# A two-layer transformer block on one core: the windowed attention's VectorE work in operations of 1024 columns, and new orders of the steps

## The reference, cut to what matters

```python
Kw = Kp[:, :, idx]                       # idx: position l sees l-3 .. l+3 (zeros beyond the ends)
scores = jnp.einsum('bhld,bhlwd->bhlw', Q, Kw) / np.float32(np.sqrt(DH))
attn = jax.nn.softmax(scores, axis=-1)
fw = attn * conn                         # conn: one weight for each head and shift, from a small network
fw = fw / (fw.sum(axis=-1, keepdims=True) + 1e-09)
out = jnp.einsum('bhlw,bhlwd->bhld', fw, Vw)
```

## Time and profile before

| | |
|---|---|
| median of 3 runs | 1133.05 us (1133.0 to 1134.91) |
| profiled execution | 1138.12 us, span 1136.3 us |
| granted TensorE clock, mean | 0.954 |
| PE busy | 1003.8 us (88%) |
| DVE busy | 943.6 us (83%), 2536 instructions |
| ACT busy | 752.2 us (66%) |

### The profile page before, as it was taken

How to read it: one execution, slowest core, us unless ns; L and a number is a source line. 1 busy time by engine, 2 the same in 40 slices (tenths; PEclk the granted TensorE clock), 3 DMA queues, 4 the chain that set the end, 5 groups by cost and what they waited for, 6 DMA issues and landing times.

```text
span 1136.3 us, 20042 instructions
## 1 busy us (share of the span) xinstructions
PE 1003.8 (88%) x7166; PEld 713.5 (63%) x7166; DVE 943.6 (83%) x2536; ACT 752.2 (66%) x1854; POOL 145.5 (13%) x400
## 2 busy tenths in 40 slices
PE   4877789999999999999999999999999898888652
PEld 2655557676867676767777676857676666565321
DVE  3877676689898989898998989998999896868854
ACT  2233554758686877768686778686877778577653
POOL 2001100101102020202011111102020202010000
PEclk8778999999999999999999999999999999999875
DMA  7821123011111202030303021120202000000000
GB/s 210 328 83 53 31 74 93 1 49 36 47 56 30 73 24 79 10 93 10 93 3 91 11 63 40 38 65 29 75 19 75 10 11 19 2 20 1 10 10 10
DMA packets 36627, 58.91 MB, mean 52 GB/s; under 512 B 6784, under 2 KB 15872, under 8 KB 36016
## 3 DMA queue, kind: packets, MB, share of 16 engines
q1 hardware_dynamic: 36528, 57.64, 16.4%
HBM read 28.65 MB, written 4.19 MB: 29 GB/s over the span
## 4 chain that ended last, share of the span: by engine, by line
PE 40%; DVE 39%; ACT 15%; issue 4%; POOL 2%; DMA 0%; SPq 0%; ACTq 0%; DVEq 0%; POOLq 0%
PE bank_c L447 15%; PE bank_e L447 6%; PE bank_a L447 5%; DVE area_f L1240 5%; DVE area_a L980 5%; DVE neg_top L1173 4%; DVE area_a L1024 3%; ACT squares_out L1314 3%; PE bank_f L447 3%; PE bank_x L447 3%; DVE x L878 2%; ACT area_e L1509 2%; DVE area_f L1231 2%; ACT area_f L1538 2%; DVE area_a L1028 2%
## 5 line engine op out<-in xcount | busy, mean ns | idle before, releaser
L1240 DVE SCALAR_TENSOR_TENSOR area_f<-area_f,w_convw 128x254 f32<-128x254 f32 x256 | 111.9, 478 | 9.3 <-ACT area_f L1538 7.0
L1302 ACT ACTIVATE area_bx<-bank_x 128x512 f32<-128x512 f32 (+1 forms) x144 | 69.9, 497 | 47.4 <-PE bank_x L641 22.0
L1173 DVE TENSOR_REDUCE neg_top<-bank_e 128x4 f32<-128x512 f32 x128 | 80.5, 681 | 10.1 <-PE bank_e L447 9.7
L1538 ACT ACTIVATE area_f<-area_f,w_convb,w_convw 128x256 f32<-128x256 f32 x128 | 69.9, 595 | 27.8 <-DVE area_f L1231 27.7
L980 DVE TENSOR_TENSOR area_a<-area_a 128x512 f32<-128x512 f32 x112 | 73.0, 682 | 14.0 <-ACT area_a L1302 13.1
L1024 DVE TENSOR_TENSOR area_a<-area_a 128x512 f32<-128x512 f32 x112 | 74.5, 684 | 0.9 <-DMA area_a<-area_a 0.7
L1302 ACT ACTIVATE area_a<-bank_a 128x512 f32<-128x512 f32 (+1 forms) x80 | 44.0, 550 | 41.2 <-PE bank_a L447 29.9
L1509 ACT ACTIVATE area_e<-bank_e 128x512 f32<-128x512 f32 x128 | 68.7, 594 | 1.4 <-PE bank_e L800 1.4
L1302 ACT ACTIVATE area_bx<-bank_c 128x512 f32<-128x512 f32 x64 | 34.5, 538 | 50.1 <-PE bank_c L447 47.6
L1028 DVE TENSOR_TENSOR area_a<-area_a 128x512 f32<-128x512 f32 x96 | 65.7, 684 | 0.2
L447 PE MATMUL bank_e<-area_e,chosen_v 128*32 128x512 f32 x256 | 57.2, 618 | 3.6 <-ACT area_e L1509 2.9
(11 more groups left out here) (307 smaller groups left out, 2716.6 us busy)
## 6 DMA issues: line engine op xcount, KB each, us to landing
area_a<-area_a SPq DMA_DIRECT2D x96, 224.0 KB
area_a<-in_xT SPq DMA_DIRECT2D x16, 256.0 KB, 2.9
x<-in_x SPq DMA_DIRECT2D x16, 256.0 KB, 2.8
area_bx<-in_ctxT SPq DMA_DIRECT2D x16, 256.0 KB, 2.7
area_d<-in_ctxT SPq DMA_DIRECT2D x16, 256.0 KB, 2.7
y<-x SPq DMA_DIRECT2D x16, 256.0 KB, 2.2
w_wqkv_e<-in_wqkv_e SPq DMA_DIRECT2D x1, 3072.0 KB, 11.0
area_f<-in_raw SPq DMA_DIRECT2D x2, 1024.0 KB, 9.9
```

The lines of the kernel that those rows point to most:

```text
L1173: dve.tensor_reduce(top[:, b, :, r, 0].rearrange("p (par c) -> p c par", c=DC), bank_e[r][:, :].rearrange("p (c par k) -> p c par k", c=DC ...
L1240: last = dve.scalar_tensor_tensor(c4[:, i, :, dst], h4[:, i, :, src], cwt3[:, 2 * jj + i, k:k + 1], c4[:, i, :, dst], ALU.mult, ALU.add)
L1302: return act.activation(dst, src, ACT.Copy)
L1538: last = act.activation(c4[:, i], h4[:, i], ACT.Identity, bias=w["convb"][:, j:j + 1], scale=cwt3[:, j, 1:2])
```

## The change

1. The five product buffers become one tile, and VectorE's products are made in four operations: shifts 0 and 2 at once, 4 and 6 at once, 1 alone, 3 and 5 at once. An operation for two shifts has 1024 columns: the queries are read twice, the keys by a pattern that begins again two positions on. PE waits for the second and the fourth of them.
2. The weighing is done in four operations (shifts 0 and 1, 2 and 3, 4 and 5, then 6), and the additions in four: a "first" of 1024 columns that adds shifts 0, 1 to 2, 3 into `prods`, one of 1024 columns for 4 and 5, one of 512 for 6, and a last that adds the two halves of 512. Each addition waits for the operation just issued ahead of it on behalf of the station.
3. `e0` is laid out by shift, sequence and head. So the sums over shifts (L1002, L1007) read with a step of 32 numbers instead of 16.
4. The order strings of all engines but POOL (where one letter pair moves) are new.

```diff
-WINDOWS = (0, 2, 4, 6, 1, 3, 5)
-SUM_STEPS = ((3,), (0,), (2,), (3, 0), (4,), (3, 2), (6,), (3, 4), (1,), (3, 6), (5,), (3, 1), (3, 5))
+PRODUCT_STEPS = ((0, 2), (4, 6), (1,), (3, 5))
+VALUE_STEPS = (("weigh", 0, 2), ("weigh", 2, 4), ("first", 0, 2), ("weigh", 4, 6), ("add", 4, 2), ("weigh", 6, 7), ("add", 6, 1),
+               ("last",))
...
-                for windows, made in ((WINDOWS[:4], 4), (WINDOWS[4:], 7)):
-                    pe.wait_ge(a_prod, WIN * g + made)
+                for windows, made in ((WINDOWS[:4], 2), (WINDOWS[4:], 4)):
+                    pe.wait_ge(a_prod, 4 * g + made)
...
+                    dve.tensor_tensor(prods[:, place:place + n, :].rearrange("p w (n t) -> p w n t", t=P),
+                                      bc(qT0.rearrange("p c (b t) -> p (c b) t", t=P), 1, n), shifted, ALU.mult).then_inc(a_prod, 1)
...
+                for step in VALUE_STEPS:
+                    if step[0] == "weigh":
+                        lo, hi = step[1:]
+                        v4 = vw[:, lo:hi, :].rearrange("p w (n d) -> p w n d", d=DH)
+                        weights = e0.rearrange("p (w n) -> p w n", w=WIN)[:, lo:hi, :]
+                        m = own.mark(dve.tensor_tensor(v4, v4, bc(weights, 3, DH), ALU.mult))
+                    elif step[0] == "first":
+                        dve.wait_ge(own.sem, m)
+                        m = own.mark(dve.tensor_tensor(prods[:, 0:2, :], vw[:, 0:2, :], vw[:, 2:4, :], ALU.add))
+                    elif step[0] == "add":
+                        lo, n = step[1:]
+                        dve.wait_ge(own.sem, m)
+                        m = own.mark(dve.tensor_tensor(prods[:, 0:n, :], prods[:, 0:n, :], vw[:, lo:lo + n, :], ALU.add))
```

More of the change, by code:

```diff
@@ L1 @@
+import itertools
 from contextlib import ExitStack
@@ L87 @@
[L87 to L91, removed]
@@ L211, in build @@
         kT0 = carve(DC * GB * LP).rearrange("p (c b t) -> p c b t", c=DC, b=GB)
-        prods = [carve(W2) for _ in range(5)]
+        prods = carve(5 * W2).rearrange("p (w n) -> p w n", n=W2)
         vw = carve(WIN * W2).rearrange("p (w n) -> p w n", w=WIN)
@@ L352, in product_of @@
         def product_of(wi):
-            return prods[WINDOWS.index(wi) % len(prods)]
+            return prods[:, WINDOWS.index(wi) % 5, :]
         block = ctx.enter_context(nc.Block())
@@ L991, in windowed @@
                 scores = bank_a[:, 0:GB * WH].rearrange("p (b w h) -> p b w h", b=GB, w=WIN)
-                e4 = e0.rearrange("p (b w h) -> p b w h", b=GB, w=WIN)
-                e_head = e4.rearrange("p b w h -> p b h w")
-                mx, den1, den2 = (den0[:, i, :].rearrange("p (b h) -> p b h", b=GB) for i in range(3))
+                e4 = e0.rearrange("p (w b h) -> p w b h", b=GB, w=WIN)
+                e_head = e0.rearrange("p (w n) -> p n w", w=WIN)
+                mx = den0[:, 0, :].rearrange("p (b h) -> p b h", b=GB)
                 m = own.mark(dve.tensor_reduce(mx, scores.rearrange("p b w h -> p b h w"), X, ALU.max))
                 dve.wait_ge(own.sem, m)
-                dve.tensor_tensor(e4, scores, bc(mx, 2, WIN), ALU.subtract).then_inc(a_shifted, 1)
+                dve.tensor_tensor(e4, scores.rearrange("p b w h -> p w b h"), bc(mx, 1, WIN), ALU.subtract).then_inc(a_shifted, 1)
                 yield
@@ L1001, in windowed @@
                 dve.wait_ge(a_exp, g + 1)
-                m = own.mark(dve.tensor_reduce(den1, e_head, X, ALU.add))
+                m = own.mark(dve.tensor_reduce(den0[:, 1, :], e_head, X, ALU.add))
                 dve.wait_ge(own.sem, m)
-                m = own.mark(dve.tensor_tensor(e0.rearrange("p (b n) -> p b n", b=GB), e0.rearrange("p (b n) -> p b n", b=GB),
-                                               bc(conn[:, :], 1, GB), ALU.mult))
+                m = own.mark(dve.tensor_tensor(e4, e4, bc(conn[:, :].rearrange("p (w h) -> p w h", w=WIN), 2, GB), ALU.mult))
                 dve.wait_ge(own.sem, m)
-                m = own.mark(dve.tensor_reduce(den2, e_head, X, ALU.add))
+                m = own.mark(dve.tensor_reduce(den0[:, 2, :], e_head, X, ALU.add))
                 dve.wait_ge(own.sem, m)
@@ L1012, in windowed @@
                 dve.wait_ge(own.sem, m)
-                dve.tensor_tensor(e4, e4, bc(mx, 2, WIN), ALU.mult).then_inc(a_fw, 1)
+                dve.tensor_tensor(e4, e4, bc(mx, 1, WIN), ALU.mult).then_inc(a_fw, 1)
                 yield
@@ L1016, in windowed @@
                 dve.wait_ge(a_fw, g + 1)
-                made = {}
-                for step in SUM_STEPS:
-                    if len(step) == 1:
-                        (wi,) = step
-                        v4 = vw[:, wi, :].rearrange("p (b h d) -> p b h d", b=GB, h=H)
-                        made[wi] = own.mark(dve.tensor_tensor(v4, v4, bc(e4[:, :, wi, :], 3, DH), ALU.mult))
-                    else:
-                        to, wi = step
-                        dve.wait_ge(own.sem, max(made[to], made[wi]))
-                        added = dve.tensor_tensor(vw[:, to, :], vw[:, to, :], vw[:, wi, :], ALU.add)
-                        if step == SUM_STEPS[-1]:
-                            added.then_inc(a_summed, 1)
-                        else:
-                            made[to] = own.mark(added)
+                for step in VALUE_STEPS:
[11 more added lines that the diff above has]
+                        m = own.mark(dve.tensor_tensor(prods[:, 0:n, :], prods[:, 0:n, :], vw[:, lo:lo + n, :], ALU.add))
+                    else:
+                        dve.wait_ge(own.sem, m)
+                        dve.tensor_tensor(prods[:, 0, :], prods[:, 0, :], prods[:, 1, :], ALU.add).then_inc(a_summed, 1)
                     yield
```

81 lines of the change are left out of this document (43 added, 38 removed).

## The result

The changed kernel took 1140.59 us (median of 7 runs, 1136.63 to 1141.18); the kernel before, beside it, 1134.43 us (1132.54 to 1136.75). The ratio is 1.0044, 95% interval 1.0030 to 1.0058: **slower by 0.44%**, 5.0 us (3.4 to 6.6), where 1130 was forecast. The medians themselves stand 6.2 us apart.

A forecast was written before the change was run, and what follows sets the result against it. PE (96% busy) and DVE (92%) were taken to bound each middle period in alternating halves. Terms -3, +1, +1, -2 gave -3 us: 1135.1 against the profiled 1138.12, so a 1130 us median; range 1124 to 1138.

The forecast's parts named there:

- hole on PE: PE ahead of C.dq, with E.aT moved behind it: up to 0.45 us open a period, at most +3.6, taken as +1.
- DVE's share: DVE over the whole run: 5.9 us less work, about half of it counting, -2 to -3.5 us, taken as -3.
- new waits on a predecessor: DVE's additions right behind what they need: 0.11 us a group, +1.8, and +1.3 us in groups 0 to 3.
- Fixed cost of an operation: DVE's column-independent cost, 0.07 us, saved when two operations become one: 0.56 us a group, 9.0 us in all.
- rival 4: DVE's merged pairs each save 0.138 us, 17.7 us in all, half on the path: 1124 us; chance 0.04.
- The new orders: Engines' step orders: win back part of PE's 27 us of idle time over 11 periods, counted as -2 us.
- a head that moves by more than 3 us: Stretch ahead of 240 us: nothing counted there, so a larger move would make the prediction wrong altogether.
- Coarser steps: Steps behind double operations on DVE: C.norm 0.26 us later, +1 over the run; E.att1 0.4 to 1.0 later, covered.
- Rival 2: PE's path: late C.norm and the open 0.45 us ahead of C.dq make it slower, 1137 up to 1141; chance 0.22.
- The period: Middle, between two F norms: 61.59 us read; 61.3 to 61.6 expected, above 61.9 would decide for slower.
- The layout of e0: DVE's sums over shifts, read with a step of 32 instead of 16: no change taken from 540 ns.

The follow-up runs named there:

- old_late: The changed kernel's merged operations in the orders of the kernel before, each merged step where its last column was worked; ratio 1.0042 to the kernel before.
- split: The changed kernel with its own orders, each 1024-column operation issued as two of 512 in the same step; ratio 1.0088 to the kernel before.
- fit: Orders of the kernel before, products and values merged only where both columns already stood side by side; ratio 1.0072 to the kernel before.
- old_early: The changed kernel's merged operations in the orders of the kernel before, each merged step where its first column was worked; ratio 1.0124 to the kernel before.

## Why the prediction was wrong

The sum was -3 (DVE) + 1 (C.norm) + 1 (hole on PE) - 2 (orders). The range ended at 1138, and 1140.59 came.

- *DVE's share, -2 to -3.5, taken as -3.* **This is the step that failed.** It netted the new waits on a predecessor (+1.8 and +1.3 us) against the merges of products and values alike (-9.0), and put half of the net on the path. The products' half arrived: -2 us of time for 3 of the 8 merges, 3.4 us of DVE. For the values the same working gives (-5 x 16 x 0.07 + 3.1) / 2 = about -1.2 us, and the run with them alone was 1.0052, **+5.9 us** (3.7 to 8.1), wide or in halves. The size of a wait was right (0.11 to 0.12), and so was their number (28 counted, 30 in the trace); the weight was wrong. They stand one behind another in the values' chain, which PE's next step for station A waits for and behind which F's last steps queue, so they cost most or all of their length (3.6 of 3.7 us, give or take 2.7; 1.6 of 2.2 in the middle), not the half of a net. The text had said that nobody on another engine waits for these but through DVE's queue. The 23 more that the changed kernel has make 2.5 us; the other 3 or so of the values' half are not explained.
- *Fixed cost of an operation, 0.07 us.* Right: spacing 1.14, DVE busy -6.0 where -5.9 stood. That rival 4's 0.138 would be wrong was right too.
- *The new orders, -2 us.* Wrong: against the old order with merged steps the new one gave 0 (1.0044 and 1.0042), though it moved much. The third norm of A starts at 121.4 and 123.2 us in its two profiles, where the second profile of before has 128.2; the granted clock from 60 to 100 us was 0.87 in after and 0.78 there, 1.00 in both from 100 to 150, so how much of the lead is the orders' is open. By the sixth norm of A the lead of 5 to 7 us is down to 2 and 0.1 (287.3 and 289.2 against 289.3), and the tail gains 2.5. The middle pays 4.6 us more than old_late's, 4.0 of it as busy time of PE. The text had named just this mark, a head that moves by more than 3 us, as one by which it would be wrong.
- *Coarser steps, C.norm 0.26 later.* In the period shown C.norm ran at 703.44 and C.dxT did not wait, as the orders were arranged around it. What was late instead was the end of the values and E.att1, counted as covered. The hole ahead of C.dq was seen right: 0.47 us, PE's waits for area_c up from 2.4 to 4.6 us in ten periods, +2.2 where +1 stood in the sum. Rival 2 came in on its sign and its time (1137 to 1141): its hole is there, its late norm is not, and most of the loss in the middle is neither. That its figure was met is in part luck.
- *The period.* 61.59 us was read from one pair of F's norms. The ten periods of the middle have 61.2 us on the mean before and 61.8 after, and single ones from 60.3 to 62.8, so the marks by one period (61.3 to 61.6, above 61.9) could not decide.
- *POOL.* The prediction lists PE, DVE, ACT and SP, and says that POOL's steps move by a letter or two. How long those 128x2 operations take depends on what DVE runs over them: the mean of the first (L1577 before) is 578 ns in the ten middle periods of the kernel before and 1118 in those of after, where one that nothing blocks takes 192. This was overlooked, but the loss of the changed kernel is not there: C's path over the scales is 0.2 us shorter than before, and split, with scales shorter still, is the slower kernel.
- *The layout of e0.* No change, as taken: 536 and 547 ns against 530 and 540. That the step of 16 is why these take longer than the 384 from PSUM was assumed; no run separates the step from the place.

What stays open: why PE is busy for 4.9 us more in the middle of the changed kernel; some 3 us of the values' half; and the middle of old_late is only 1.1 us longer than before's, its time 5.7 us by the medians. Part of that rest is in direct waits of the first five groups (17 of its 30), the other part in a head whose clock differs from one execution to the next, which single profiles don't resolve.

## What to carry to other kernels

Merge operations where the result goes to another engine in any case and nothing fine stands behind them (the products), and not inside a chain whose links need each other: there each merge brings the links closer, and a direct wait at 0.11 us costs more than a merge saves at 0.07. Before widening an operation of VectorE with two inputs in SBUF, look at what GpSimd has to do under it, and whether that is on the path: in fit and old_early it was, in the changed kernel it was not. And when a new order gains at the head, measure the middle by itself. The best kernel of this study is the one with the products alone merged, 1131.3 and 1132.8 us against 1134.2 and 1134.4; the interval of the second run just reaches 1 (1.0002).

## What the chip showed that was not expected

- A 128x2 operation of GpSimd takes 192 ns alone and up to the whole length of VectorE's 1024-column operation, 1.17 us, under it. It is free under one that reads PSUM.
- A sum right behind the operation that it needs starts 0.11 to 0.12 us later than one with any other operation between. With 34 such places more the program was 3.6 us longer, give or take 2.7.
- A TENSOR_SCALAR of 1024 columns in SBUF takes 685 ns, as long as a TENSOR_TENSOR of 512 (683), and blocks GpSimd all the same.
